# Graph attention by exactly sorted edges: 281 straight-line gathers, segment scans along the free axis, carries through TensorE

## The reference, cut to what matters

```
h = (x_flat @ W_gat).reshape(M, HEADS, NUM_EXPERTS)          # 4 heads x 4 experts
a_src = (h * att_src).sum(-1)
a_dst = (h * att_dst).sum(-1)
e = jax.nn.leaky_relu(a_src[src] + a_dst[dst], negative_slope=0.2)
e_max = jax.ops.segment_max(e, dst, num_segments=M)
ee = jnp.exp(e - e_max[dst])
denom = jax.ops.segment_sum(ee, dst, num_segments=M)
alpha = ee / (denom[dst] + 1e-16)
msg = h[src] * alpha[:, :, None]
agg = jax.ops.segment_sum(msg, dst, num_segments=M).reshape(M, HEADS * NUM_EXPERTS) + b_gat
```

## Time and profile before

| | us |
|---|---|
| median of 3 runs | 4744.22 |
| span of the profiled execution | 5102.1 |
| stage `so`, ranking the routing's edges | 118.75 to 231.4 |
| stage `es` with scatter `sa` | 231.4 to 650 |
| stage `f0` with scatters `sb` and `sc` | 1687 to 2724 |
| stage `gt`, the routing | 3605.9 to 4712.1 |
| stage `f1` | 4712.7 to 5087 |

### The profile page before, as it was taken

One profiled execution on the slowest core, in us unless ns is written; L12 is line 12 of the kernel. 1 busy time (PEld: TensorE's weight loads), 2 busy tenths in 40 slices (PEclk: granted clock), 3 DMA queues, 4 the chain that ended last, 5 costly groups with the idle time before them and its releaser, 6 DMA issues. The chain is left out here.

```text
span 5102.1 us, 58668 instructions
## 1 busy us (share of the span) xinstructions
PE 2674.1 (52%) x11127; PEld 1856.8 (36%) x11128; DVE 1893.5 (37%) x4714; ACT 1149.0 (23%) x3778; POOL 2164.1 (42%) x2734
## 2 busy tenths in 40 slices
PE   3223945665542399999203777774100001635898
PEld 2123923333321277777102333333100000423676
DVE  5600265656557711111002222223444445465411
ACT  0010022222210111111001111111466666310111
POOL 0165045555530665565562666660466665000000
PEclk8555556666655699999656666665555555555999
DMA  2111422222220000000001333330000000000000
GB/s 71 40 41 60 181 55 76 79 78 76 72 59 0 25 10 17 9 20 1 1 1 41 90 88 88 90 90 17 5 5 5 5 5 4 0 0 11 19 9 25
DMA packets 118123, 199.51 MB, mean 39 GB/s; under 512 B 54417, under 2 KB 81158, under 8 KB 115910
## 3 DMA queue, kind: packets, MB, share of 16 engines
q0 software_dynamic: 75360, 124.95, 10.1%
q1 hardware_dynamic: 42726, 74.12, 4.2%
HBM read 186.58 MB, written 12.36 MB: 39 GB/s over the span
## 5 line engine op out<-in xcount | busy, mean ns | idle before, releaser
L493 POOL DMA_INDIRECT a0rows<-table,a0idx x462 | 469.6, 1016 | 517.6 <-ACT a0idx L478 403.8
L493 POOL DMA_INDIRECT a1rows<-table,a1idx x444 | 421.5, 949 | 325.3 <-ACT a1idx L478 175.5
L950 POOL DMA_INDIRECT erecords<-sc_slot x416 | 408.5, 982 | 328.3 <-POOL sc_slot L946 311.7
L523 PE MATMUL a1ps<-a1rows,a1w 128*128 128x256 f32 x888 | 428.1, 605 | 191.9 <-DMA a1rows<-table,a1idx 135.3
L523 PE MATMUL a0ps<-a0rows,a0w 128*128 128x257 f32 x924 | 416.3, 585 | 177.0 <-DMA a0rows<-table,a0idx 82.7
L1146 POOL DMA_INDIRECT gt_land<-table_gat,gt_idx x324 | 356.8, 1101 | 249.9 <-POOL gt_idx L1141 162.2
L1341 ACT ACTIVATE gt_parts<-gt_nb,gt_land 128x128 f32 x1296 | 414.8, 392 | 20.7 <-DVE gt_parts L1191 1.8
L1363 PE MATMUL gt_psT<-k_ident,gt_top 128*128 128x128 f32 x100 | 27.9, 434 | 702.2 <-DVEq L1196 702.2
L749 PE MATMUL f0dn<-f0w,f0hid 128*128 128x256 f32 x1600 | 353.3, 380 | 61.9 <-DVE k_x L797 61.9
L523 PEld LDWEIGHTS a1ps<-a1rows,a1w 128*128 128x128 f32 x888 | 212.0, 279 | 408.1 <-issue 283.5
L764 PE MATMUL f0up<-k_xnT,f0w 128*128 128x320 f32 x1280 | 352.9, 435 | 12.8 <-DMA f0b<-in_f_b 12.8
(11 more groups left out here) (366 smaller groups left out, 4185.1 us busy)
## 6 DMA issues: line engine op xcount, KB each, us to landing
es_ea<-in_eaT SPq DMA_DIRECT2D x16, 1664.0 KB
es_lane<-lane_row SPq DMA_DIRECT2D x16, 832.0 KB
f0w<-in_f_W SPq DMA_DIRECT2D x16, 512.0 KB
a0rows<-table,a0idx POOLq DMA_INDIRECT x462
a1rows<-table,a1idx POOLq DMA_INDIRECT x444
erecords<-sc_slot POOLq DMA_INDIRECT x416
table<-k_tbl SPq DMA_DIRECT2D x10, 650.0 KB, 3.5
gt_land<-table_gat,gt_idx POOLq DMA_INDIRECT x324
```

Of the source, the lines that this page charges most:

```text
L493: pool.indirect_dma_start(rows[:, i, 0:TW], None, table, bass.IndirectOffsetOnAxis(ap=idx[:, i:i + 1], axis=0)).then_inc(gathered[i], 16)
L523: nc.tensor.matmul(sum_of(t), w[:, i, :], rows[:, i, 0:width], start=False, stop=False).then_inc(agg_done, 1)
L950: pool.indirect_dma_start(self.rec_dram, bass.IndirectOffsetOnAxis(ap=slot[:, i, 0:1], axis=0), slot[:, i, 1:R + 1], None).then_inc(self.p ...
```

## The change

The routing's edges are now sorted exactly by destination node. `emit_rank_edges` with the tag `so` is replaced by `emit_sort_edges`. It has two phases, and both are written out without loops. The first counts: for each of 256 chunks DVE makes one-hot lanes (eight chunks to an instruction), TensorE multiplies them with one-hot tiles to a 128x25 count, ACT moves the counts to SBUF; 25 running sums over the chunks and a few small operations turn the counts into the first free slot for every node and chunk, kept as two bf16 halves (`parts`). The second looks up: in 32 pieces of 8 chunks, SP loads the edges' lanes and tiles as rows, DVE compares them to lane numbers, and TensorE does four products per chunk: one that looks up the start slot (`psl`), and three that add up, for every pair of edges of a chunk, 1 for the same lane, 1 for the same tile and 1 for an earlier place (`pse`); ACT takes relu(x - 2) and sums it along the row, which is the edge's rank within its chunk and node.

Every node's edge to itself becomes a record with the `SELF` bit, so there are 32768 + 3200 slots, 281 to a partition (`GJ`), node by node. Records are one int32 instead of two, and there are 288 columns (`GREC`) to scatter instead of 256: `sa` takes 176 as before, `sb` 112 instead of 80.

`emit_routing` keeps all 281 gathered columns in SBUF. POOL issues the 281 gathers straight from `source`, 16 in flight at most, with no copies. Maximum, mass and messages are then scans along the 281 slots of each partition, and what flows from one partition to the next is carried by transposes through TensorE (`carry_over`, three times). The scanned array goes to DRAM (`gstate`, 3.45 MB), and 25 more gathers read each node's last slot.

```diff
-BL = 4
...
-GBLOCKS = GE // (BL * P) + NT
-GS = GBLOCKS * BL
+GSLOTS = GE + NP
+GJ = GSLOTS // P
+GREC = -(-GJ // 8) * 8
+GRING = 16
+SELF = 1 << 14
...
+def emit_sort_edges(nc, S, A):
...
+    B1, PC = 8, 8
+    PIECES = GC // PC
...
+            for q in range(PIECES):
+                if q >= 2:
+                    sp.wait_ge(transposed_hot, q - 1)
+                cols = slice(q * PC * P, (q + 1) * PC * P)
+                sp.dma_start(row_lane[:, q % 2, :], lane_row[:, cols].to_broadcast([P, PC * P])).then_inc(row_in[q % 2], 16)
+                sp.dma_start(row_tile[:, q % 2, :], tile_row[:, cols].to_broadcast([32, PC * P])).then_inc(row_in[q % 2], 16)
...
+            for b in range(GC // B1):
+                if b >= 2:
+                    v.wait_ge(counted, b - 1)
+                nc.vector.tensor_tensor(hot_lane[:, b % 2, :, :],
+                                        lanef[:, b * B1:(b + 1) * B1].unsqueeze(2).to_broadcast([P, B1, P]),
+                                        S.iota[:, 0:P].unsqueeze(1).to_broadcast([P, B1, P]), ALU.is_equal).then_inc(lanes_hot, 1)
+            v.wait_ge(evicted, GC // B1)
+            for t in range(NT):
+                nc.vector.tensor_tensor_scan(before[:, t, 1:GC + 1], before[:, t, 1:GC + 1], zero[:], 0.0, ALU.add, ALU.add)
...
+            nc.vector.tensor_tensor(before[:, :, 0:GC], before[:, :, 0:GC], base[:].unsqueeze(2).to_broadcast([P, NT, GC]), ALU.add)
+            v.drain()
+            nc.vector.tensor_copy(parts[:, :, 0, :].rearrange("p c t -> p t c"), before[:, :, 0:GC])
+            v.drain()
+            nc.vector.tensor_tensor(parts[:, :, 1, :].rearrange("p c t -> p t c"), before[:, :, 0:GC],
+                                    parts[:, :, 0, :].rearrange("p c t -> p t c"), ALU.subtract)
+            v.drain().then_inc(split, 1)
...
+            def one_hots(q):
+                v.wait_ge(row_in[q % 2], 32 * (q // 2) + 32)
+                if q >= 2:
+                    v.wait_ge(looked, (q - 1) * PC // 8)
+                    v.wait_ge(compared, (q - 1) * PC // 4)
+                nc.vector.tensor_scalar(hot_lane_t[:, q % 2, :], row_lane[:, q % 2, :], S.lane[:, 0:1], None, ALU.is_equal)
+                nc.vector.tensor_scalar(hot_tile_t[:, q % 2, :], row_tile[:, q % 2, :], S.lane[0:32, 0:1], None, ALU.is_equal)
+                v.drain().then_inc(transposed_hot, 1)
+
+            one_hots(0)
+            for q in range(PIECES):
+                if q + 1 < PIECES:
+                    one_hots(q + 1)
+                for a in range(PC // 8):
+                    k = q * PC // 8 + a
+                    v.wait_ge(looked, k + 1)
+                    nc.vector.tensor_tensor(picked[:].rearrange("p c (k t) -> p c k t", k=2),
+                                            psl[:, k % 2, 0:8 * 2 * NT].rearrange("p (c k t) -> p c k t", c=8, k=2),
+                                            hot_tile[:, k * 8:k * 8 + 8, :].unsqueeze(2).to_broadcast([P, 8, 2, NT]), ALU.mult)
+                    v.drain().then_inc(look_taken, 1)
+                    nc.vector.tensor_reduce(look[:, k * 8:k * 8 + 8], picked[:], AX.X, ALU.add)
...
+            for c in range(GC):
+                b, i = divmod(c, B1)
+                if i == 0:
+                    pe.wait_ge(lanes_hot, b + 1)
+                    if b >= 2:
+                        pe.wait_ge(evicted, b - 1)
+                ins = nc.tensor.matmul(psc[:, b % 2, i * NT:(i + 1) * NT], hot_lane[:, b % 2, i, :], hot_tile[:, c, :],
+                                       start=True, stop=True)
+                if i == B1 - 1:
+                    ins.then_inc(counted, 1)
...
+                ins = nc.tensor.matmul(psl[:, k % 2, j * 2 * NT:(j + 1) * 2 * NT], lane_t,
+                                       parts[:, c, :, :].rearrange("p k t -> p (k t)"), start=True, stop=True)
+                if j == 7:
+                    ins.then_inc(looked, 1)
+                g, j = divmod(c, 4)
+                if j == 0 and g >= 2:
+                    pe.wait_ge(compare_taken, 4 * (g - 1))
+                same = pse[:, g % 2, j * P:(j + 1) * P]
+                nc.tensor.matmul(same, lane_t, lane_t, start=True, stop=False)
+                nc.tensor.matmul(same, tile_t[0:NT, :], tile_t[0:NT, :], start=False, stop=False)
+                ins = nc.tensor.matmul(same, trib[:], S.identb[:], start=False, stop=True)
+                if j == 3:
+                    ins.then_inc(compared, 1)
...
+                nc.scalar.copy(before[:, :, 1 + b * B1:1 + (b + 1) * B1],
+                               psc[:, b % 2, 0:B1 * NT].rearrange("p (c t) -> p t c", t=NT)).then_inc(evicted, 1)
...
+                same = pse[:, g % 2, j * P:(j + 1) * P]
+                nc.scalar.activation(same, same, ACT.Relu, bias=minus2[:, 0:1], accum_out=within[:, c:c + 1]).then_inc(compare_taken, 1)
...
+            pool.wait_ge(unpacked, 1)
+            for j in range(J):
+                turn, lane = divmod(j, GRING)
+                if turn:
+                    pool.wait_ge(gathered[lane], 16 * turn)
+                pool.indirect_dma_start(land[:, j, :], None, S.table_gat,
+                                        bass.IndirectOffsetOnAxis(ap=source[:, j:j + 1], axis=0)).then_inc(gathered[lane], 16)
+            pool.wait_ge(saved, 16)
+            for t in range(NT):
+                turn, lane = divmod(t, GRING)
+                if turn:
+                    pool.wait_ge(drawn[lane], 16 * turn)
+                pool.indirect_dma_start(sums[:, t, :], None, S.gstate,
+                                        bass.IndirectOffsetOnAxis(ap=S.gend[:, t:t + 1], axis=0)).then_inc(drawn[lane], 16)
...
+            sp.wait_ge(kept, 1)
+            sp.dma_start(S.gstate.rearrange("(p j) k -> p j k", p=P), land[:]).then_inc(saved, 16)
+            sp.wait_ge(saved, 16)
...
+            def carry_over(round_, n, op0, op1, at_first):
+                v.drain().then_inc(packed, 1)
+                v.wait_ge(turned, round_ + 1)
+                nc.vector.tensor_copy(turned_sb[0:n, 0, :], psT[0:n, 0:P])
+                nc.vector.tensor_copy(turned_sb[0:n, 1, :], psT[0:n, P:2 * P])
+                nc.vector.memset(carry[0:n, 0:1], at_first)
                 v.drain()
+                nc.vector.tensor_tensor_scan(carry[0:n, 1:P + 1], turned_sb[0:n, 1, :], turned_sb[0:n, 0, :], at_first, op0, op1)
+                v.drain().then_inc(scanned, 1)
+                v.wait_ge(returned, round_ + 1)
+                nc.vector.tensor_copy(init[:, 0:n], psR[:, 0:n])
...
+            for h in range(H):
+                nc.vector.tensor_tensor_scan(best[:, h, :], keep[:], best[:, h, :], 0.0, ALU.mult, ALU.add)
...
+            for f in range(GW):
+                h = f // HC if f < HW else f - HW
+                nc.vector.tensor_tensor_scan(state[:, f, :], decay[:, h, :], state[:, f, :], 0.0, ALU.mult, ALU.add)
+            for h in range(H):
+                nc.vector.tensor_tensor_scan(best[:, h, :], decay[:, h, :], zero[:], 1.0, ALU.mult, ALU.add)
...
+                nc.vector.scalar_tensor_tensor(land[:, :, f], best[:, h, :], init[:, f:f + 1], state[:, f, :], ALU.mult, ALU.add)
...
-            emit_rank_edges(nc, S, "so", GC, BL, A["gsrc"], A["gdst"], None, GS, recg, rec_dram, S.granges)
+            emit_sort_edges(nc, S, A)
...
-            beside = (Scatter(nc, S, "sb", recg, rec_dram, EARLY, GC, S.rec_sb, stage),
+            beside = (Scatter(nc, S, "sb", recg, rec_dram, EARLY, GREC, S.rec_sb, stage),```

POOL's list in the routing. Before, where the loop over blocks stands (`gt_idx` is the copied index column, `gt_land` the four slots):

```order
L1136 UNCONDITIONAL_BRANCH
L1136 ISA
L1140 REGISTER_ALU
L1141 ISA
L1141 COPY gt_idx<-k_rec 128x1
L1146 DMA gt_land<-table_gat,gt_idx 128x20
```

More of the change, by code:

```diff
@@ L1267, in _ @@
[L1267 to L1268 removed]
+            nc.vector.reciprocal(den[:], den[:])
             v.drain()
[L1270 to L1274 removed]
```

461 lines of the change are left out of this document (226 added, 235 removed).

## The result

The kernel after takes 4337.62 us (median of 4, 4332.57 to 4342.24) where the one before takes 4745.63 (4 runs, 4742.98 to 4748.11): ratio 0.9136, 95% interval 0.9123 to 0.9149, 408 us less. Forecast were 4320 us, range 4235 to 4420.

A forecast was written before the change was run, and what follows sets the result against it. Each touched stage was taken to have its own limit: DVE in ranking, POOL ending the experts, gather-by-gather chain in routing. -611 + 62 + 105 = -444 us gave 4300, or 4331 if everything shrinks alike; forecast 4320 us, range 4235 to 4420.

The forecast's parts named there:

- Routing: Term for the whole routing stage: 1107 us go, 496 us stand in their place, a gain of 611 us.
- 281 x 1.27 = 357: Routing step: 281 gathers at the 1.27 us pitch of the scatters in `es`, 357 us, bounds 273 to 401.
- DVE ... Sum 70 us: Routing step: scans, elementwise work, exponentials, carries, drains and small copies take 70 us, bounds 55 to 95.
- Store: Routing step: storing 3372 KB of scanned states to DRAM takes 15 us, bounds 10 to 25.
- Both rivals on their price: Routing gathers: 1.6 us or so each in bulk, about 4415 us (7%); or only POOL's 0.97, about 4230 us (8%).
- Scatters: Term for `sb` beside the experts: 32 more columns at 1.93 us, not hidden, +62 us, bounds 41 and 70.
- The sort: Term for sorting the edges: 218 us (97 + 115 + 6) against 113, +105 us, bounds +65 to +195.
- Then three passes over 6400 elements at 6.8 are 20: End of the sort's first phase: three passes at 6.8 us each, 20 us of about 97.
- I take 0.45 us per chunk: Sort's second phase: between TensorE's 0.5 and ACT's estimates, 0.45 us per chunk, 115 us for 256.
- The sum: All stages: -611 routing + 62 scatters + 105 sort = -444 us, profiled span 5102.1 to 4658 us.
- The sign named as one of error: Whole kernel: span falls by 444 us but median by much less, if the unprofiled routing was shorter all along.
- Straight-line code starves: Rival: the sort's 1282 written-out products (or 281 gathers) delivered every 2.85 us, adding 3650 us, about 7900; 3%.

The follow-up runs named there:

- e1: The kernel before, unchanged, profiled a second time: 4745.76 us, span 4745.0.
- e8: The kernel after with two row gathers in flight instead of 16, on a late chip: 4738.26 us.
- e7: The kernel after with one row gather in flight instead of 16, on a late chip: 5130.27 us, ratio to before 1.0029.
- e2: The kernel after with both halves of the look-up table written contiguously and read by TensorE with a step: 4315.12 us.
- e3: The kernel after with the product adding the mask of earlier edges made once for four chunks: 4338.5 us, no change.
- e5: The kernel after with one product over 114 rows for the two over 128 and 25, late chip: 4680.52 us against after's 4737.28.
- e10: The kernel after with e2, e5, `f0` scatters written out without copy, and 16 `es` scatters moved to `f0`; late chip: 4941.3 us, ratio 0.9649.
- e11: e10 with GpSimd's copy kept ahead of each written-out `f0` scatter, same late chip: 4413.16 us, ratio 0.8628.
- e12: e11 with the 160 scatters of `es` also spaced by GpSimd's copy, on a prompt chip: 3974.87 us, ratio 0.8375.

## Why the prediction was right, and where it was not

The direction, the stages and the order of sizes were right: 4337.6 in a range of 4235 to 4420. That it came within 18 us of the forecast is in part luck, as the sum below shows.

- *Routing*, "496 us": between the prediction's own ends, first DMA to `f1`'s first load, it is 3454.87 to 3940.57, 485.7 us; the 491.1 of the row above reach to `f1`'s first product, 6 us later. Gathers "281 x 1.27 = 357": 351. "DVE ... Sum 70 us": 74, its pieces off in both directions: scans took 0.64 us rather than 0.76, and reading the landed rows with a step of 96 bytes was dearer, 2.95 us for 1124 elements (1.34 said) and 11.3 for 4496 (4.8 said), 2.5 to 2.6 ns an element, as was writing them back, 0.71 us for 281 (0.46 said). Store "15": 9.6. The gain was 630 rather than 611, half of it for these 10 us and half because the routing of before takes 1116.6 us in e1's profile and not 1107; why it does no run shows.
- *Gathers*: that GpSimd's issue sets the pitch once two are in flight is shown by e8, and that those in flight hide the landing by e7. Both rivals on their price are out.
- *Scatters*, "+62": +61. `es` "as long as before": 239 and 240 us, once like is set beside like.
- *The sort*, "+105 us": +160, the mis-sized term. Two steps of it failed. "Then three passes over 6400 elements at 6.8 are 20": 6.8 + 15.3 + 29.4 = 51.6; e2 shows that the step in the table is the cause (both passes write with it, and the second reads with it too). "I take 0.45 us per chunk": 0.58; the row of four products in 0.60 was read as 0.15 each, and e3 and e5 show 0.11 for a product among full-height ones and 0.21 beside one of 25 rows. 0.5, "if that figure is taken whole", was the better reading. ScalarE was 0.34, near the 0.32 of its nearest row, and its second operation overlaps: 0.34 is the pitch of the pair. Nothing faster than that row is seen, and the prediction was right not to count on it. The 55 us of error are these 31 and 0.13 x 256 = 33, less 9 elsewhere.
- *The sum*, -444, was 36 us too large: 55 too little for the sort, 19 too little gain for the routing, which cancel in part. The forecast missed by only 18 because it stood 20 above 4744 - 444, for a reason that was itself wrong: the touched stages are no shorter unprofiled. Both are luck.
- *"The median of the runs is 357.9 us below the span of before, and no view tells where"*: by its stages it was a late chip's profile beside a prompt chip's times. The sign named as one of error, a span that fell by 444 us and a median that fell by much less, did not come as stated: the span fell by 771 us, and the two agree once before is profiled on a prompt chip (4745.0 - 4330.8 = 414).
- *"Straight-line code starves"*, 3%: it did not happen in the kernel after, whose sort takes 274 us on a prompt chip and on a late one, and its ground, "the slow delivery goes away with the scatters", held. The price of 2.85 us was read from one pair of products: the earlier trace rows has 480 in those 251 us, one in 0.52, so the rival would have cost some 670 us rather than 3650, as an estimate. e10 comes near the higher price (2.8 us on average) where dense scatters and products meet, and e11 shows that code without loops is not enough to cause it. The Trainium skill, "Runtime: NRT & Kernel Launch", instruction fetch mechanics, has straight-line code fetched ahead, at a cost that is mostly hidden. The runs agree for the sort, where 1282 products are written out and the second phase keeps TensorE busy for 50 of 50 us; they don't show what delays `f0`'s products on a late chip, which stand in a loop.

What stays open: what makes a chip late; what GpSimd's issue and TensorE's instructions share; whether the distance between scatters or the copy between them helps; and whether in `es` and the aggregates spacing would repay itself on such chips.

## What to carry to other kernels

A profile and the times beside it may come from different chips: where a span is far from the median, profile the same kernel again before any term is taken from it, and compare stages that the edit leaves alone. A stage that GpSimd sets by its number of indirect DMAs is shortened by writing them out without a copy (typically 1.97 to 1.26 us each, 335 us here), and gathers lose only 9 us with two in flight (e8). But on a late chip that edit cost more than it gave. The one form measured that kept most of the gain on both kinds has GpSimd's copy ahead of each scatter, some 1.5 us apart (e11 on a late chip, e12 on a prompt one). Lay a table out as it is written when the writer is VectorE with 2-byte elements (24 us here), and try to do without a product of few rows between full-height ones (54 us here).

## What was not expected of the hardware

- Two kinds of chips or sessions: the same kernel takes 4746 or 5118 us, each within 0.5%. On the late kind, in `f0`, TensorE gets one product in 2.8 us on average while scatters are issued 1.27 us apart with nothing between them, few delays with a copy between them and 1.48 us on average, none at 1.97.
- bfloat16 written with a step of 100 bytes: 15.3 us (copy) and 29.4 us (two inputs, one of them read with that step) for 6400 elements, against 6.8 when contiguous.
- A bfloat16 product of 128 columns at 1.2 GHz costs its columns, about 0.11 us (e5: 306 columns in 0.25), in a row of full-height ones and 0.21 ahead of one of 25 rows, which costs 0.21 as well.
- ACTIVATE with a sum output on 128x128 from PSUM to PSUM: 0.34 us in a row, the read of the accumulator (0.20) overlapped.
